# Spreading a per-node score to all partitions through memory instead of by TensorE transposes, with new instruction orders on every engine

## What is computed

```
h = x @ W_fc.T;  f1 = h @ a1;  f2 = h @ a2
scores = leaky_relu(f1[:, None] + f2[None, :], 0.2), masked with -1e9 where adj == 0
h1 = elu(softmax(scores) @ x)
x  = layernorm(x + h1)
xn = x / |x|;  out = layernorm(x + ((xn @ xn.T) @ adj) @ x)
```

## Time and profile before

| | |
|---|---|
| median of 3 runs | 341.21 us (339.38 to 342.82) |
| the profiled execution | 339.95 us, span from first to last instruction 338.1 us |
| PE busy | 318.5 us, 94% of the span |
| PE weight load busy | 301.3 us, 89% |
| ScalarE busy | 293.3 us, 87% |
| VectorE busy | 287.0 us, 85% |
| GpSimd busy | 210.3 us, 62% |
| mean granted TensorE clock | 0.99 |

### The profile page before, as it was taken

How to read it: one execution, slowest core, us unless ns; L and a number is a source line. 1 busy time by engine, 2 the same in 40 slices (tenths; PEclk the granted TensorE clock), 3 DMA queues, 4 the chain that set the end, 5 groups by cost and what they waited for, 6 DMA issues and landing times.

```text
span 338.1 us, 7382 instructions
## 1 busy us (share of the span) xinstructions
PE 318.5 (94%) x2418; PEld 301.3 (89%) x2418; DVE 287.0 (85%) x1013; ACT 293.3 (87%) x610; POOL 210.3 (62%) x238
## 2 busy tenths in 40 slices
PE   6778899999989999999999999999999999999992
PEld 3577799989889999999999999999999998998881
DVE  2889999999788989989898989989898989856635
ACT  1589989999699999999999999999999999993561
POOL 4340493877447666675967676676958676665623
PEclk9979999999999999999999999999999999999998
DMA  8633461560715455264464454363464462210122
GB/s 237 201 88 104 123 186 25 166 186 8 240 37 156 124 151 163 71 181 124 126 181 130 127 157 156 81 186 111 138 174 128 131 177 67 65 62 0 44 73 74
DMA packets 33494, 41.93 MB, mean 124 GB/s; under 512 B 1168, under 2 KB 25264, under 8 KB 33456
## 3 DMA queue, kind: packets, MB, share of 16 engines
q0 software_dynamic: 16416, 24.64, 26.6%
q1 hardware_dynamic: 16944, 16.78, 15.9%
q10 hardware_dynamic: 96, 0.03, 0.0%
HBM read 33.06 MB, written 8.39 MB: 123 GB/s over the span
## 4 chain that ended last, share of the span: by engine, by line
PE 79%; DVE 10%; POOL 4%; issue 3%; ACT 2%; DMA 1%; POOLq 0%; ACTq 0%; DVEq 0%
PE ps_l L1208 14%; PE ps_l L1168 9%; PE ps_l L1169 8%; PE ps_h L1138 8%; PE ps_h L1139 7%; PE ps_h L1140 7%; PE ps_probT L1122 6%; PE ps_l L1194 4%; PE ps_l L1196 4%; PE ps_l L1195 4%; PE ps_l L1180 4%; PE ps_f L1111 2%; DVE score L453 1%; DVE product L432 1%; DMA wfc<-w_fc 1%
## 5 line engine op out<-in xcount | busy, mean ns | idle before, releaser
L1138 PE MATMUL ps_h<-x_hi,probT_hi 128*128 128x256 f32 x256 | 78.8, 308 | 7.6 <-POOL x_lo L263 2.3
L1139 PE MATMUL ps_h<-x_lo,probT_hi 128*128 128x256 f32 x256 | 72.0, 281 | 0.0
L1140 PE MATMUL ps_h<-x_hi,probT_lo 128*128 128x256 f32 x256 | 72.0, 281 | 0.0
L1168 PE MATMUL ps_l<-xn_hi,adj_sb 128*128 128x256 f32 x256 | 64.0, 289 | 0.8 <-POOL xn_lo L304 0.5
L1208 PE MATMUL ps_l<-w_sb,xnT 128*128 128x256 f32 x256 | 62.5, 380 | 0.8 <-ACT w_sb L873 0.6
L1169 PE MATMUL ps_l<-xn_lo,adj_sb 128*128 128x256 f32 x256 | 62.5, 283 | 0.0
L304 POOL TENSOR_TENSOR xn_lo<-xn,xn_hi 128x1024 fp32r<-128x1024 f32 x15 | 36.0, 2400 | 38.6 <-ACT xn_hi L843 38.6
L1138 PEld LDWEIGHTS ps_h<-x_hi,probT_hi 128*128 128x128 f32 x256 | 48.6, 190 | 12.1 <-DVE probT_lo L484 9.0
L798 ACT ACTIVATE score<-score,f 128x512 f32<-128x512 f32 x64 | 44.4, 726 | 8.7 <-DVE row_max L453 8.6
L1168 PEld LDWEIGHTS ps_l<-xn_hi,adj_sb 128*128 128x128 f32 x256 | 48.8, 191 | 2.4 <-DVE y L560 0.9
L1208 PEld LDWEIGHTS ps_l<-w_sb,xnT 128*128 128x128 f32 x256 | 45.1, 189 | 6.5 <-issue 1.9
(11 more groups left out here) (78 smaller groups left out, 794.9 us busy)
## 6 DMA issues: line engine op xcount, KB each, us to landing
adj_sb<-adj POOLq DMA_DIRECT2D x15, 1024.0 KB, 5.9
x_sb<-x SPq DMA_DIRECT2D x16, 512.0 KB, 4.7
x_hi<-x POOLq DMA_DIRECT2D x15, 512.0 KB, 4.1
out<-o_sb SPq DMA_DIRECT2D x15, 512.0 KB, 3.2
adj_sb<-adj POOLq DMA_DIRECT2D x4, 256.0 KB, 4.6
out<-o_sb SPq DMA_DIRECT2D x4, 128.0 KB, 1.7
wfc<-w_fc ACTq DMA_DIRECT2D x1, 32.0 KB, 3.8
attn_cols<-w_attn ACTq DMA_DIRECT2D x1, 0.2 KB, 2.9
```

The costliest lines, as they stand in the source:

```text
L1138: nc.tensor.matmul(ps, probT_hi[:, c, blk], x_hi[n][:, k, :], start=(k == 0), stop=False)
L1139: nc.tensor.matmul(ps, probT_hi[:, c, blk], x_lo[n][:, k, :], start=False, stop=False)
L1140: last = nc.tensor.matmul(ps, probT_lo[:, c, blk], x_hi[n][:, k, :], start=False, stop=(k == NC - 1))
L1168: nc.tensor.matmul(ps, a, xn_hi[n][:, k, :], start=(k == 0), stop=False)
```

## The change

f2 of graph 0 is still spread by four PE transposes (`bcast_first`). From graph 1 on, SP writes the 512 values of `f[:, 1, :]` to a 2 KB buffer in device memory (one element at a time, since neighbours in a partition are 128 nodes apart), waits until they have landed, and loads the row back into all 128 partitions of `f2_row` (two buffers). ScalarE's `put_f2` copies that row into `ps_f2`, where `masked_f2` reads it as before.

ScalarE makes the mask and `x_hi` of graph 0. POOL takes over the second half of `residual_part` (`residual_sum_part`). The load of `wfc` is first in SP's list instead of second in ScalarE's. The lists of all engines are new. The core of the diff:

```diff
+    f2_mem = nc.dram_tensor("f2_mem", [2, N], F32, kind="Internal").ap()
+        f2_row = [sb(f"f2_row{n}", [P, N], F32) for n in range(2)]
...
+            def f2_through_memory(g):
+                if not graph(g) or g == 0:
+                    return
+                n, m = g % NBUF, g % 2
+                sp.wait_ge(f2_ok, g + 1)
+                if f2_uses(g) > 1:
+                    sp.wait_ge(f2_row_in[m], 16 * (f2_uses(g) - 1))
+                sp.dma_start(f2_mem[m].rearrange("(c p) -> p c", p=P), f[n][:, 1, :],
+                             allow_slow_non_contiguous=True).then_inc(f2_out[m], 16)
+                sp.wait_ge(f2_out[m], 16 * f2_uses(g))
+                if f2_uses(g) > 1:
+                    sp.wait_ge(f2_bcast, g - 1)
+                sp.dma_start(f2_row[m][:], f2_mem[m].partition_broadcast(P)).then_inc(f2_row_in[m], 16)
...
+            sp.dma_start(wfc[:], w_fc).then_inc(wfc_in, 16)
+
             load_x(0)
             load_x(1)
+            f2_through_memory(1)
             load_x(2)
+            f2_through_memory(2)
...
             for i in range(3, B - 2):
-                load_x(i + 2)
-                store(i - 2)
+                store(i - 3)
+                f2_through_memory(i + 2)
+                load_x(i + 3)
...
+            def residual_sum_part(c):
+                pool.wait_ge(q_ok, c + 1)
+                pool.tensor_tensor(y[0][:, c, :], y[0][:, c, :], exp_h[:, c, :], ALU.add).then_inc(y_ok, 1)
...
+            def split_x_hi():
+                act.wait_ge(x_in[0], 16)
+                nc.scalar.activation(x_hi[0][:], x_sb[0][:], ACT.Copy).then_inc(x_hi0_ok, 1)
+
+            def make_mask_part(c):
+                act.wait_ge(adj0_in[c], 16)
+                nc.scalar.activation(mask[:, c, :], adj_sb[0][:, c, :].bitcast(F32), ACT.Copy, bias=-MASKED,
+                                     scale=MASKED).then_inc(mask_ok, 1)
...
+            def put_f2(g):
+                if not graph(g) or g == 0:
+                    return
+                m = g % 2
+                act.wait_ge(f2_row_in[m], 16 * f2_uses(g))
+                if graph(g - 1):
+                    act.wait_ge(score_ok, NC * g)
+                nc.scalar.activation(ps_f2[:], f2_row[m][:], ACT.Copy).then_inc(f2_bcast, 1)
```

More of the change, by code:

```diff
@@ L125, in program @@
         x_lo_ok = sem("x_lo_ok")
+        f2_out = [sem(f"f2_out{n}") for n in range(2)]
+        f2_row_in = [sem(f"f2_row_in{n}") for n in range(2)]
         f2_bcast = sem("f2_bcast")
@@ L670, in _ @@
             residual2(0, 1)
-            residual2(0, 2)
             masked_f2(3, 0)
             masked_f2(3, 1)
[L674 to L685, removed]
-            for i in range(3, B - 2):
+            for i in range(3, B - 2):
+                masked_f2(i, 2)
+                residual2(i - 3, 2)
+                residual2(i - 3, 3)
+                masked_f2(i, 3)
+                z_lo_part(i - 2, 0)
+                negate_max(i, 0)
+                node_scores(i + 1, 1)
+                negate_max(i, 1)
+                residual(i - 1)
+                z_lo_part(i - 2, 1)
+                z_lo_part(i - 2, 2)
+                z_lo_part(i - 2, 3)
+                probT_lo_part(i, 0)
                 probT_lo_part(i, 1)
@@ L689, in _ @@
                 denominators(i)
+                row_moments2(i - 3)
                 probT_lo_part(i, 2)
+                normalise(i - 1)
                 node_scores(i + 1, 0)
+                residual2(i - 2, 0)
                 probT_lo_part(i, 3)
-                residual2(i - 2, 0)
-                normalise(i - 1)
+                masked_f2(i + 1, 0)
                 residual2(i - 2, 1)
-                masked_f2(i + 1, 0)
                 masked_f2(i + 1, 1)
[L698 to L712, removed]
+            residual2(B - 5, 2)
+            masked_f2(B - 2, 2)
+            masked_f2(B - 2, 3)
+            residual2(B - 5, 3)
+            z_lo_part(B - 4, 0)
+            negate_max(B - 2, 0)
+            node_scores(B - 1, 1)
+            negate_max(B - 2, 1)
+            residual(B - 3)
+            z_lo_part(B - 4, 1)
+            z_lo_part(B - 4, 2)
+            z_lo_part(B - 4, 3)
+            probT_lo_part(B - 2, 0)
+            row_moments2(B - 5)
             probT_lo_part(B - 2, 1)
             row_moments(B - 3)
+            denominators(B - 2)
+            probT_lo_part(B - 2, 2)
             node_scores(B - 1, 0)
-            probT_lo_part(B - 2, 2)
-            probT_lo_part(B - 2, 3)
             normalise(B - 3)
@@ L928, in _ @@
             elu_relu(1, 0)
-            probT_hi_part(1, 2)
-            probT_hi_part(1, 3)
-            lrelu(2, 0)
             elu_exp(1, 1)
@@ L935, in _ @@
             xn_hi_first(1)
+            put_f2(2)
             xn_hi_first(2)
@@ L1062, in _ @@
-                lrelu(i + 3, 1)
-                elu_exp(i + 2, 2)
+            softmax_exp(B - 1, 1)
+            probT_hi_part(B - 1, 0)
+            scale_z(B - 3, 1)
+            scale_z(B - 3, 2)
+            probT_hi_part(B - 1, 1)
+            scale_z(B - 3, 3)
+            lrelu(B - 1, 2)
+            lrelu(B - 1, 3)
+            softmax_exp(B - 1, 2)
+            softmax_exp(B - 1, 3)
+            probT_hi_part(B - 1, 2)
+            probT_hi_part(B - 1, 3)
+            copy_xnT(B - 3, 0)
```

398 lines of the change are left out of this document (189 added, 209 removed).

## The result

The changed kernel takes 429.7 us in the median of 4 runs (427.8 to 431.3), the kernel before 340.3 us beside it: a ratio of 1.26, 95% interval [1.25, 1.27]. That is 89 us more, where 6 less was forecast, and far outside the range.

A forecast was written before the change was run, and what follows sets the result against it. PE was taken to bound the loop at 18.87 us a round. Prologue -1.1, two transposes -0.9 and loop -4.4 summed to -6.4 us, giving 334.5 us, range 329.5 to 341.5.

The forecast's parts named there:

- The bound: Loop: PE, busy for the whole 18.87 us round, sets the period, with ScalarE 0.6 us behind.
- The value of the transposes: Loop: 0.44 us a round leaves PE; with some waits 0.40 us saved, 4.4 us over 11 rounds.
- `put_f2` at 0.50 us: ScalarE in the loop: the added copy of 512 elements a round costs 0.50 us.
- ScalarE's load: Loop: ScalarE's round with the new copy, 18.2 us counted from start to start, under PE's 18.43.
- my two readings: ScalarE's round with the new copy: 18.75 us by busy share, 18.2 us by adding starts to next starts.
- ScalarE takes PE's place: Loop rival: period 18.77 to 18.87 us, time 338 to 339.5; chance 0.2, shared with a late prologue.
- the trip costs nothing in the loop: Loop: f2's way through memory takes 7.7 us, 4 us inside its 11.8 us budget, so it hides.
- The slower rival: At `put_f2`: too long a trip stalls ScalarE each round, then PE; about 338 to 366 us; chance 0.13 with misfitting lists.
- Its formula: Loop: the round is the trip plus 6.6 us for the rest of its circle, decisive from 11.8 us.
- The prologue: Start, up to `make_z(0, 0)`: reached at 38.5 instead of 39.63, a gain of 1.1 us.
- the gaps go too: Rival, prologue and near 83.5 us: new lists also close 3 to 4 us of PE gaps, 330.5 us; chance 0.2.
- The lists: Middle, 83.5 to 102.4 us: new instruction orders may open or close gaps; counted as nothing, 1 us either way.

The follow-up runs named there:

- the mended lists: The changed kernel's instruction orders with f2 spread by transposes in every graph, `x_hi` loaded before the adjacency and x after it landed: 335.2 us, ratio 0.984.
- the slow `make_z`: Three kernels with four neighbouring nodes to a partition, column blocks read with a step of four: transposes 393.6 us, trip through memory 394.1, four f2 copies 395.5.
- the kernel with the dear parts of the trip taken out: Changed kernel with `x_hi` loaded before the adjacency, 16-byte write, row from many places in x after the adjacency (wrong values): 338.1 us, ratio 0.992.
- the run at a distance of 64 bytes: Changed kernel with its 512 4-byte pieces written 64 bytes apart and the row read from many places in x (wrong values): 343.1 us, ratio 1.006.
- the lists: Changed kernel's instruction orders on all engines, but f2 of every graph spread by transposes, no transfer through memory, no `put_f2`: 347.1 us, ratio 1.01.
- the mend on the changed kernel: Changed kernel, f2 still written 4 bytes at a time side by side, with only `x_hi` moved before the adjacency and x after it: 431.6 us, ratio 1.27.

## Why the prediction was wrong

**The bound: right. The value of the transposes: not borne out.** PE was the bound, and in the mended lists it still is, at 18.8 us a round. But no kernel without the transposes gained the forecast 0.40 us a round: the best rounds gained 0.14, and with the slow `make_z` it was 0.2.

**`put_f2` at 0.50 us: right** (0.52 from its start to the next, 208.07 to 208.59). **ScalarE's load: mis-sized.** I put 18.2 us a round on it, and took PE's 18.43 for the bound. The shortest rounds without a wait show 18.6 us for ScalarE, between my two readings. The rival "ScalarE takes PE's place" fits better: the kernel with the dear parts of the trip taken out lands at 338.1 us, inside its 338 to 339.5.

**The step that failed: "the trip costs nothing in the loop".** It priced the trip by its own landing and asked only who waits for the row. The landing was wrong, 9.1 + 7.6 us instead of 3.2 + 3.5; I took the store's 3.2 us since it has as many pieces. The runs show that neither the number of the pieces nor their size alone sets it: 512 pieces of 4 bytes land in 2.0 us at a distance of 64 bytes, 128 of 16 bytes side by side in 1.7, and only pieces of 4 bytes side by side hold the DMA engines for 9. But the larger fault is the question left out: what stands behind it on the shared engines. In the loop `put_f2` waited 1.2 us in all; the mask waited 4.9 a round, since the adjacency has some 7 us of room and needs 12.

**The slower rival: right in its sign, wrong in its place.** It named `put_f2` as the place, but the trace has ScalarE waiting at `make_mask`. Its formula, with the measured trip of 16.7 us, gives 23.3 us a round, and 24.7 were measured. That is luck, since the formula is about a wait that hardly occurred. The highest time that it named was 366 us. Its chance, 0.13, was too low: the range of the trip was drawn from rows of large pieces only, and the one row with small ones, `attn_cols`, has 64 words.

**The skill's rule** (the Trainium skill, "DMA: Bandwidth & Descriptors", Rules for kernel authors: a strided last dimension makes one descriptor per element) warned in the right direction. The trace agrees that there was one piece per element, 505 in the microsecond shown. My reading of its Specifications, that so small a piece is slow as such, the run at a distance of 64 bytes does not bear out, at 2.0 us for all 512.

**The prologue: right without the trip, wrong with it.** 1.1 us was forecast, the mended lists give 1.9, and the gaps near 83.5 us, which I counted at nothing, close with them as the rival "the gaps go too" had it. The trip at the start took 16.6 us (14.11 to 30.68), and the mark came 13.7 us late.

**The lists: counted at nothing, and a cost of 1 us a round in the profiled execution.** I checked them for ScalarE's and VectorE's work and not for which loads run together. Adjacency, `x_hi` and x were now issued within 3.6 us.

In sum, the 89 us, each part given by the ratios and by the medians, in the order in which the runs peel them off: the lists 4 or 7 us (the first not clear of the noise); the reads of one place 19 or 20; the pieces side by side 63 or 61; the rest of the trip between -4 and +4, by whether the 16-byte or the distant pieces stand for it. In another order the parts would differ, as the mend on the changed kernel shows.

## What to carry to other kernels

A transfer is priced twice: by its own landing, and by what is queued behind it on the same DMA engines. The second price fell on a load that has nothing to do with it. Pieces of 4 bytes should not be written next to each other from many partitions (64 bytes apart, or as 16-byte pieces, they cost little here), and a row that all partitions need should not be read 128 times from one place, where it can be had otherwise. When an order is changed, list for each large load what else is issued within its landing time: moving two loads by some microseconds was worth 9 to 12 us here, more than the transposes are worth at most, 0.44 us in each of 15 graphs.

## What the runs showed of the hardware

Pieces of 4 bytes written side by side to device memory cost 113 us over 15 graphs more than the same pieces 64 bytes apart (460.0 and 346.7 us). 512 bytes written so, in 128 pieces, cost 72 us (440.4, one execution, against 368.4 without them), as much as the 2 KB. Pieces of 16 bytes side by side do not do it: 128 of them land in 1.7 us. That the DMA engines wait for each other on a shared stretch of memory is my explanation; the runs show the dependence on distance and on the size of a piece, and not the mechanism. Distances between 4 and 64 bytes were not tried.

128 reads of 2 KB from one address cost 20 us over 15 rows against reads from different ones (368.4 and 348.7 us), where other loads ran beside them. Alone, behind the adjacency, such a row landed in 3.8 us.

Fp32r weights read with a step of four elements (16 bytes) load in 328 ns instead of 191, and the matmuls that use them start 0.23 us apart instead of 0.12.
